# A transformer block in one kernel: where the second maxima stand between score tiles, and a middle stage with 128 rows

## The reference

```
x1 = x  + tanh(g0) * perceiver_attention(LN(LN x) -> queries, keys over 2048 tokens and 1601 context rows)
x2 = x1 + tanh(g2) * mixture_of_experts(LN x1)        # 8 experts of width 128, top 2
x3 = x2 + tanh(g1) * cross_attention(LN x2, context)  # 16 heads of 16
out = x3 + tanh(g3) * quantised_gated_ffn(LN x3)
```

## Time and profile before

| | us |
|---|---|
| median of 3 runs (3391.16 to 3396.19) | 3391.27 |
| profiled execution | 3392.96 |
| its span | 3391.1 |
| TensorE busy | 3001.4 (89%) |
| VectorE busy | 2453.9 (72%) |
| GpSimd busy | 2082.1 (61%) |
| ScalarE busy | 1817.4 (54%) |

### The profile page before, as it was taken

One profiled execution on the slowest core, in us unless ns is written; L12 is line 12 of the kernel. 1 busy time (PEld: TensorE's weight loads), 2 busy tenths in 40 slices (PEclk: granted clock), 3 DMA queues, 4 the chain that ended last, 5 costly groups with the idle time before them and its releaser, 6 DMA issues. The chain is left out here.

```text
span 3391.1 us, 53618 instructions
## 1 busy us (share of the span) xinstructions
PE 3001.4 (89%) x21696; PEld 1101.4 (32%) x21704; DVE 2453.9 (72%) x3029; ACT 1817.4 (54%) x2033; POOL 2082.1 (61%) x968
## 2 busy tenths in 40 slices
PE   3589999999999999999999999998697799999947
PEld 1223333333333333333333333322354133333324
DVE  5567777778767877778777876782535888888758
ACT  3155445555555545544555555544443588888833
POOL 0077898888888889879888888989510111111022
PEclk9699999999999999999999999999698799999969
DMA  1000000000000000000000000000210100000000
GB/s 59 5 1 1 1 7 1 1 1 7 1 1 7 1 1 7 1 1 7 1 1 1 2 1 1 1 1 1 74 23 13 42 7 6 7 8 6 4 0 26
DMA packets 24536, 28.72 MB, mean 8 GB/s; under 512 B 6431, under 2 KB 21216, under 8 KB 24290
## 3 DMA queue, kind: packets, MB, share of 16 engines
q1 hardware_dynamic: 24290, 25.30, 2.6%
HBM read 17.42 MB, written 2.10 MB: 6 GB/s over the span
## 5 line engine op out<-in xcount | busy, mean ns | idle before, releaser
L413 POOL TENSOR_TENSOR a_acc_p<-a_acc_p,a_prob 128x1024 f32<-128x1024 f32 x704 | 1726.1, 2452 | 299.5 <-ACT a_prob L483 217.8
L543 DVE TENSOR_REDUCE a_part_max<-wide 128x2 f32<-128x1024 f32 x896 | 1088.4, 1215 | 475.6 <-PE wide L713 474.9
L483 ACT ACTIVATE a_prob<-slot,a_mask_bias 128x1024 f32<-128x1024 f32 x928 | 987.6, 1113 | 732.1 <-PE slot L738 712.7
L753 PE MATMUL bank<-a_prob,a_val 128*64 128x512 f32 x3712 | 898.8, 606 | 2.1 <-ACT a_prob L483 2.1
L713 PE MATMUL wide<-a_k_hi,a_q_hi 64*128 64x512 f16 (+1 forms) x2048 | 365.9, 369 | 147.4 <-DVE a_part_max L543 134.9
L1025 ACT ACTIVATE a_prob<-slot,a_mask_bias 128x1024 f32<-128x1024 f32 x416 | 455.4, 1116 | 65.5 <-PE slot L1183 52.2
L1067 DVE TENSOR_REDUCE a_part_max<-wide 128x1 f32<-128x512 f32 x514 | 332.7, 681 | 37.3 <-PE wide L1171 20.4
L753 PEld LDWEIGHTS bank<-a_prob,a_val 128*64 128x64 f32 x3712 | 226.6, 136 | 394.9 <-issue 290.2
L738 PE MATMUL slot<-a_q_hi,a_k_lo 64*128 64x512 f16 x1856 | 353.1, 377 | 0.0
L738 PE MATMUL slot<-a_q_hi,a_k_step_hi 64*128 64x512 f16 x1728 | 328.7, 377 | 2.6 <-ACT a_prob L483 2.5
L738 PE MATMUL slot<-a_q_lo,a_k_step_hi 64*128 64x512 f16 x1728 | 328.3, 377 | 0.0
(11 more groups left out here) (367 smaller groups left out, 3284.6 us busy)
## 6 DMA issues: line engine op xcount, KB each, us to landing
a_w_staged<-in_w SPq DMA_DIRECT2D x8, 384.0 KB, 3.2
x_res<-in_x SPq DMA_DIRECT2D x1, 2048.0 KB, 9.1
a_q_op<-a_hi SPq DMA_DIRECT2D x128, 16.0 KB, 1.8
out_x<-x_res SPq DMA_DIRECT2D x16, 128.0 KB
a_k_op<-mid_k_hi SPq DMA_DIRECT2D x32, 52.0 KB, 2.2
mid_context<-in_ctxt SPq DMA_DIRECT2D x1, 1601.0 KB, 6.6
mid_w_staged<-in_w1a SPq DMA_DIRECT2D x4, 385.0 KB, 4.2
ctx_rows<-in_ctx SPq DMA_DIRECT2D x1, 1536.0 KB
```

What stands on the lines that cost most here:

```text
L413: nc.gpsimd.tensor_tensor(acc, before, prob[:, k % R, :], ALU.add).then_inc(added_p, 1)
L483: nc.scalar.activation(prob[:, k % R, :], m.slot[k % 2][:, :], ACT.Exp, bias=mbias[:, t:t + 1]).then_inc(probs_ready, 1)
L543: nc.vector.reduce_max(part_max[:, w % 2, :, j, c], pairs, AX.X).then_inc(max_used, 1)
L753: ins = nc.tensor.matmul(av[r, :], val[g % 2][:, t, r], prob[:, k % R, h * QB:(h + 1) * QB], start=(t == 0), stop=(t == NT - 1), tile_posi ...
```

## The change

It has two parts.

In the first attention TensorE's order in odd tiles becomes scores, sums, outputs, turn, projection, pair, values. VectorE's duties move: the inversions to tiles 10, 11, 13, 15, the division to 17, the outputs (and their residuals behind them) to tiles 19 and 21, and the tiles that VectorE adds become 4, 6, 14, 16, 22.

```diff
-        self.sums_at, self.invert_at, self.pieces, self.divide_at, self.out_at = 9, 12, 4, 16, (17, 19)
+        self.sums_at, self.invert_at, self.divide_at, self.out_at = 9, (10, 11, 13, 15), 17, (19, 21)
+        self.pieces = len(self.invert_at)
         self.last_pair, self.turn_at = 24, 25
-        self.dve_tiles = [5, 7, 9, 15, 17]
+        self.dve_tiles = [4, 6, 14, 16, 22]
...
-                    if w and 0 <= t - a.invert_at < a.pieces:
-                        invert(w - 1, t - a.invert_at)
+                    if w and t in a.invert_at:
+                        invert(w - 1, a.invert_at.index(t))
...
                     scores(w, t)
-                    if n < S:
-                        pair(n)
-                    if t == 1:
-                        for s in (NT - 2, NT - 1) if w else ():
-                            values(w - 1, s)
-                    else:
-                        for s in range(t - 3, t if t == NT - 2 else t - 1):
-                            values(w, s)
                     if w and t == a.sums_at:
                         sums(w - 1)
...
                     if w * NT + t in a.job_at:
                         project(*a.job_at[w * NT + t])
+                    if n < S:
+                        pair(n)
+                    if t == 1:
+                        for s in (NT - 2, NT - 1) if w else ():
+                            values(w - 1, s)
+                    else:
+                        for s in range(t - 3, t if t == NT - 2 else t - 1):
+                            values(w, s)
```

```diff
-        self.jobs = [(g, kind, c) for g in range(self.groups) for kind in "kv" for c in range(len(self.chunks))]
+        kinds = [("k", 0)] + [("v", g) for g in range(self.groups)] + [("k", g) for g in range(1, self.groups)]
+        self.jobs = [(g, kind, c) for kind, g in kinds for c in range(nc)]
...
-        ones = sb("ones", [2, P], FP16)
-        y = sb("kv_y", [P, a.y_ring, 512])
+        ones = sb("ones", [P, 512], FP16)
...
-        wt_h, wt_l = sb("wt_hi", [NE, TOK], FP16), sb("wt_lo", [NE, TOK], FP16)
-        pick = sb("pick", [NE, NE, P], FP16)
+        wt_h, wt_l = sb("wt_hi", [P, TOK], FP16), sb("wt_lo", [P, TOK], FP16)
+        pick = sb("pick", [P, NE, P], FP16)
...
+            sp.dma_start(bias[:, :, :].rearrange("p k c -> p (k c)"), bias_in[0:1, :].broadcast_to([2, 2 * a.groups * P])).then_inc(bv_loaded, 16)
+            sp.dma_start(w_st[:, 1, :], w_in[1, :, :]).then_inc(w_loaded[1], 16)
             for dst, source in fetch[a.small:]:
                 sp.dma_start(dst, source).then_inc(fetched, 16)
-            sp.dma_start(bias[:, :], bv_in[0:1, :].broadcast_to([2, a.groups * P])).then_inc(bv_loaded, 16)
...
+            nc.gpsimd.memset(bias_op[:, :, :], 0.0).then_inc(bias_chain, 1)
             nc.gpsimd.memset(ones[:, :], -1.0).then_inc(bias_chain, 1)
+            nc.gpsimd.memset(wt_h[:, :], 0.0).then_inc(wt_zeroed, 1)
+            nc.gpsimd.memset(wt_l[:, :], 0.0).then_inc(wt_zeroed, 1)
...
-            for g in range(1, a.groups):
-                for p in k_jobs[NC * g:NC * (g + 1)]:
-                    k_low(p)
+            for g in range(a.groups):
                 ones_of(g)
...
-                nc.scalar.activation(y[:, k % a.y_ring, 0:w], jbank(p)[:, 0:w], ACT.Identity, bias=b, scale=1.0 / WSCALE).then_inc(y_set, 1)
-                nc.scalar.activation(k_hi[:, g % 2, at:at + w], jbank(p)[:, 0:w], ACT.Identity, bias=b, scale=1.0 / WSCALE).then_inc(evacuated, 1)
+                nc.scalar.activation(k_hi[:, g % 2, at:at + w], jbank(p)[:, 0:w], ACT.Copy, scale=1.0 / WSCALE).then_inc(evacuated, 1)
...
+            def k_low(p):
+                g, _, c = a.jobs[p]
+                at, w = a.chunks[c]
+                dve.wait_ge(evacuated, p + 1)
+                if g >= 2:
+                    dve.wait_ge(laid[g % 2], a.laid_group * (g // 2))
+                nc.vector.scalar_tensor_tensor(k_lo[:, g % 2, at:at + w], jbank(p)[:, 0:w], 1.0 / WSCALE, k_hi[:, g % 2, at:at + w],
+                                               ALU.mult, ALU.subtract).then_inc(k_split, 1)
...
+                    ins = nc.tensor.matmul(out[:, 0:w], own_bias, ones[:, 0:w], start=False, stop=True)
```

More of the change, by code:

```diff
@@ L1308, in keep_for_cross, with stage_middle @@
     keep.val = [sb(f"val{g}", [P, NCT, P]) for g in range(a.groups)]
-    keep.w_hi = sb("w_hi", [P, a.groups, 3 * DC * P], FP16)
-    keep.w_lo = sb("w_lo", [P, a.groups, 3 * DC * P], FP16)
-    keep.qk_bias = sb("qk_bias", [P, a.groups, 2])
+    keep.wq_hi, keep.wq_lo = sb("wq_hi", [P, a.groups, DC * P], FP16), sb("wq_lo", [P, a.groups, DC * P], FP16)
+    keep.q_bias = sb("q_bias", [P, a.groups])
     return keep
-def stage_middle(nc, m, gate, weights, fetch, context, w_in, bv_in, keep):
+def stage_middle(nc, m, gate, weights, fetch, context, w_in, bias_in, keep):
     a = Middle()
@@ L1448, in _ @@
             c_split(3)
+            w_split(1)
+            w_split(2)
+            for e in range(NE):
+                nc.gpsimd.tensor_copy(pick[:, e, :], m.ident[:, e:e + 1].broadcast_to([P, P])).then_inc(picked, 1)
             e_split(1)
-            w_split(1)
-            for p in range(0, NC):
-                k_low(p)
+            w_split(3)
             e_split(2)
             e_split(3)
-            ones_of(0)
-            w_split(2)
-            w_split(3)
-            for g in range(1, a.groups):
-                for p in k_jobs[NC * g:NC * (g + 1)]:
-                    k_low(p)
+            for g in range(a.groups):
                 ones_of(g)
@@ L1543, in _ @@
             evacuate(4)
-            e_high(2)
-            evacuate(5)
-            e_high(3)
-            evacuate(6)
             act.wait_ge(shifted, 1)
             nc.scalar.activation(flat(lg), flat(lg), ACT.Exp).then_inc(exp_done, 1)
+            evacuate(5)
+            evacuate(6)
+            w_high(2)
             evacuate(7)
-            w_high(2)
             evacuate(8)
+            e_high(1)
+            w_high(3)
             evacuate(9)
-            w_high(3)
-            for p in range(10, 14):
+            evacuate(10)
+            e_high(2)
+            evacuate(11)
+            evacuate(12)
+            e_high(3)
+            for p in range(13, NC + a.routing):
                 evacuate(p)
@@ L1558, in _ @@
                 weights_high(g)
-                evacuate(14 + g)
-            for p in range(14 + NB, a.nj):
+                evacuate(NC + a.routing + g)
+            for p in range(NC + a.routing + NB, a.nj):
                 evacuate(p)
@@ L1626, in _ @@
             scale(0, 2)
+            dve.wait_ge(bias_chain, 3)
+            link(nc.vector.tensor_scalar(bias[:, :, :], bias[:, :, :], WSCALE, None, ALU.mult))
+            link(nc.vector.tensor_copy(bias_hi[:, :, :], bias[:, :, :]))
+            nc.vector.scalar_tensor_tensor(bias_op[0:2, :, :], bias_hi[:, :, :], m.ident[0:2, 1:2], bias[:, :, :], ALU.mult, ALU.subtract).then_inc(bias_ready, 1)
             x_low(0, 1)
@@ L1629, in _ @@
             x_low(0, 2)
+            k_low(0)
             x_low(0, 3)
             link(nc.vector.tensor_scalar(tgs[:, :], m.tg[:, gate:gate + 1], 1.0 / WSCALE, None, ALU.mult))
[L1632 to L1635 removed]
+            for p in range(1, NC):
+                k_low(p)
             dve.wait_ge(routed, NB)
@@ L1804, in _ @@
                 route(b)
-            for p in range(4, 12):
+            for p in range(NC, NC + a.routing):
                 project(p)
-            first(0)
-            first(1)
-            project(12)
-            project(13)
             pe.wait_ge(weights_done, 1)
@@ L1817, in _ @@
                 ins.then_inc(wt_turned, 1)
-                project(14 + g)
-            for p in range(14 + NB, a.nj):
+                project(NC + a.routing + g)
+            first(0)
+            first(1)
+            for p in range(NC + a.routing + NB, a.nj):
                 project(p)
```

102 lines of the change are left out of this document (44 added, 58 removed).

## The result

The changed kernel takes 3458.64 us (median of 4 runs, 3457.77 to 3459.36), the kernel before 3391.22 beside it: ratio 1.0195, 95% interval 1.0177 to 1.0213. It is 67 us slower; the forecast was 39 us slower, in a range of 3385 to 3466.

A forecast was written before the change was run, and what follows sets the result against it. TensorE, busy in 89% of the span, was taken to bound the kernel, waiting in the first attention on VectorE's maximum. 3391.3 + 42 (first attention) - 3 (middle stage) = 3430 us, range 3385 to 3466.

The forecast's parts named there:

- the forecast case: Whole kernel: slower by waits on the bank `side`, 3400 to 3458 us, chance 0.58.
- Part 1 (order): First attention, odd tiles: moved matmuls cover 29 of 48 losses of 0.19 before pairs, saving 5.5 us per group.
- Part 2 (side waits): First attention: moved matmuls wait for VectorE's readers of the bank `side`, costing 12.7 us per group.
- 0.10 + D: First attention: TensorE's wait per moved matmul, D being the reader's duration, 0.74 residual, 0.69 key chunk, 0.68 query chunk.
- Part 3 (duties): First attention: VectorE's moved duties delay pairs less, gaining 1.0 us per group; bounds a gain of 7.3, a loss of 3.1.
- Last group: First attention's group without projections: three late outputs 1 (2.5) less 9 covered losses (1.7), +0.8 us.
- Part 4 (middle): Middle stage: start, key bias, clock and low halves together -3 us (-14 to +8).
- clock terms: Middle stage: 128 rows hold TensorE's clock, half of the first drop and all of the second returning, -3.3 and -3.4 us.
- key bias: Middle stage: key projections get their bias by a matmul, +2.9 us.
- The start: Middle stage: earlier bias load against new memsets and a wider bias chain on the path, -1 us (-4 to +4).
- The faster case: First attention: side waits only rename the pair's wait; middle 3345 us, about 3385 with half the side waits; chance 0.16.
- The slower one: First attention: adds of 2.2 or more and pair 26 late in every unit, 3463 us; chance 0.18.

The follow-up runs named there:

- experiment 1: The kernel before with only the new first attention, 3469.54 us (ratio 1.0227), and with only the new middle stage, 3380.40 us (0.9964).
- half_old: mid_only with GpSimd adding only half the columns of each probability tile, the other half's sums left out: 3302.14 us (ratio 0.9729).
- half_early: readers_early with GpSimd adding only half the columns of each probability tile, the other half's sums left out: 3305.69 us (ratio 0.9740).
- proj_ahead: mid_only with only sums, turn and projections moved ahead of pair, outputs left behind values, projections read in the same tile: 3384.28 us (ratio 0.9974).
- experiments 2 and 4: 2: changed kernel with earlier readers or TensorE's old order, 3386.05 and 3394.58 us; 4: GpSimd adding half the columns in three kernels, 3383.44, 3302.14 and 3305.69.
- old_order: The changed kernel with TensorE's pair and values back in front of sums, outputs, turn and projection, new duty tiles kept: 3394.58 us (ratio 1.0004).
- mid_only: The kernel before with the new middle stage alone, its first attention unchanged: 3380.40 us (ratio 0.9964).
- few_rows: mid_only with bias matmuls of keys and values back to 2 rows, gate and expert-bias matmuls back to 8: 3395.65 us (ratio 1.0005).
- bias_2rows: mid_only with only the bias matmuls of keys and values back to 2 rows of contraction instead of 128: 3394.27 us (ratio 1.0016).
- readers_early: The changed kernel with VectorE's projection evacuation and residual add moved one tile forward, into the tile of their matmuls: 3386.05 us (ratio 0.9979).

## Why the prediction was right, and where it was off

The direction, the main mechanism and its size were right; 28 us of the total were missing, in terms that partly cancel. By the two runs of the parts it was 34 in the attention, less the 10 that the middle stage gained beyond its forecast (the 4 us left are the spread named under experiment 1). That they cancel is luck: the measured +76 with the forecast -3 would have been 3464, at the edge of the range, and 3458.64 lies just above the 3400 to 3458 that I gave the forecast case.

- **Part 1 (order).** -5.5 per group: the losses in front of odd pairs went as counted (with GpSimd's half adds, 14.7 to 8.3 us between `half_old` and `half_early`, 0.8 more than the 5.5, which I put down to duties). Missing was the price of moving: 0.10 for the change of tile at each of 36 places per group. At 16 of them it is inside the waits of part 2; at the other 20 it adds 2.0, and the sums add 0.4. `proj_ahead` shows the net of such a move as zero.
- **Part 2 (side waits).** Forecast 12.7, each wait 0.10 + D. Measured 0.84 a wait and 15.1 - 2.0 = 13.1 per group; moving the readers takes 10.3 to 11.4 of it away (the 16 changes of tile stay). Right in place and size.
- **Part 3 (duties).** Forecast -1.0 with bounds -7.3 and +3.1. Of the excess of before, 22.1, some 9.1 are the 48 losses and 2.7 tile 0, so duties had 10.3; after, 10.8 at even pairs and 8.3 - 3.6 - 2.7 = 2.0 at odd ones: +2.5, near the upper bound. I had kept the low half at 0.8; it met GpSimd's adds in its new neighbourhood and doubled (0.87 to 1.81), while adds fell from 2.29 to 1.74, below my 1.9. The sum is then -5.5 + 2.0 + 0.4 + 13.1 + 2.5 = 12.5, for 12.7 measured. It closes because all terms come from one tally of the trace; experiments 2 and 4 check the side waits and GpSimd's part by themselves. The duties were isolated in the old order alone, where they cost 3.6 (`old_order` against `mid_only`).
- **Last group.** Forecast +0.8, measured -6.1. With GpSimd's adds whole, the kernels with the new duty tiles have 186.5 to 187.4, those with the old ones 192.2 to 194.7: where no projection and no low half stand in the same tiles the new duties are worth some 2 us a unit. Why was not tested. I had priced only the outputs there.
- **Part 4 (middle).** Forecast -3, measured -13. The clock terms (-6.7 forecast) came as 6.9 and 1.7. The large missing term is the change of tile: -11 for the value blocks, and some -5 for the 8 rows of the gate and the expert bias (171.7 us in `few_rows` and 163.1 in `bias_2rows` from the first projection to the last expert step: 8.6, of which 3.4 are the dip). Against them +2.9 for the key bias as forecast, and two new gaps, 4.31 for the last key halves on VectorE and 1.7. The start did not gain: TensorE's first projection waited 6.0 for the bias operand, the chain that I had put on the path. (A VectorE scaling alone takes 0.40 in the trace and not my 0.35; the sum did not use it.) From the first projection to the last expert step: 172.4 before, 156.6 in `mid_only`; some 3 of these 16 are lost again later, where I did not look. That the clock at the first dip came back because of 128 rows is not shown: it stays at 1.00 with 2 rows too.
- **Rivals.** The faster case (waits renamed) is refuted by `readers_early` and `old_order`. The slower one (3463) gave nearly this time, but by late pairs with adds of 2.2; the adds were shorter and the low halves longer.

## What to carry to other kernels

When a matmul is moved ahead of others, move the reader of its bank with it, or count one wait per reuse: two readers, one tile earlier, were worth 72 us of 78. Price a reordering on TensorE by its neighbours as well: a change of rows or columns between matmuls cost 0.10 us each way here, and two of them eat a covered loss of 0.19. Where VectorE and GpSimd both take two SBUF inputs, the rest of the other engine's instruction comes on top of one's own, so make the long one's pieces shorter while it has time to spare.

## What the runs showed of the hardware that was not expected

- A VectorE operation with two SBUF inputs stands until GpSimd's running instruction ends and then does its own work: 8 columns took 0.16 with GpSimd idle and 1.36 on average, and an add of 1.22 took the rest of GpSimd's instruction and 1.08 in all 115 cases of the kernel before. The Trainium skill names the contention (GPSIMD Engine Reference, Specifications) and gives no price; here it is up to one GpSimd instruction, 2.4 us. A scaling with one SBUF input was held longer: one of the four in the earlier trace rows took 8.49 us (the shortest 0.40), from 2409.26 until 0.15 behind the end of five GpSimd instructions without a gap (2413.41 + 4.19 = 2417.60). VectorE's operations with one input in PSUM beside it kept their length (residual 0.74, key chunk 0.60 on average in `before`, `after`, `readers_early` and `proj_ahead`).
- A matmul whose rows or columns differ from its neighbour's starts 0.10 us later: 64 to 128 rows (0.31 for 0.215), 128 to 2 and back (0.60 for 0.39 a block), 64 to 128 columns at 128 rows (0.53 for 0.43).
- 2-row matmuls between full ones kept the clock at 1.00 here; the first dip of the kernel before is not explained by them, and its cause stays open.
